# Attention of a decoder layer: turned heads split once and regrouped into stacks by SBUF transfers

## The reference

```python
kv = ln(x, kvn_w, kvn_b) @ kv_w + kv_b              # 16 heads of 32, keys and values
q  = ln(x, qn_w, qn_b) @ q_w + q_b
q, k = rotary(q, x, rh_w, rh_b), rotary(k, x, rh_w, rh_b)   # scaled by a radius that depends on the row
qn, kn = ln(q, ln_w, ln_b), ln(k, ln_w, ln_b)        # over the 32 of a head
attn = softmax(einsum('bhqd,bhkd->bhqk', qn, kn) / sqrt(32))
x1 = x + einsum('bhqk,bhkd->bhqd', attn, v) @ out_w + out_b
```

## Time and profile before

| | us |
|---|---|
| median of 3 runs | 2368.12 (2367.32 to 2368.73) |
| time of the profiled execution | 2366.49 |
| its span, from first to last instruction | 2364.7 |
| mean granted clock of PE over the span, as a share | 0.926 |

### The profile page before, as it was taken

How to read it: one execution, slowest core, us unless ns; L and a number is a source line. 1 busy time by engine, 2 the same in 40 slices (tenths; PEclk the granted TensorE clock), 3 DMA queues, 4 the chain that set the end, 5 groups by cost and what they waited for, 6 DMA issues and landing times. The chain is left out here.

```text
span 2364.7 us, 31908 instructions
## 1 busy us (share of the span) xinstructions
PE 1990.4 (84%) x10328; PEld 1432.6 (61%) x10328; DVE 1609.8 (68%) x3007; ACT 1061.1 (45%) x1820; POOL 1025.8 (43%) x879
## 2 busy tenths in 40 slices
PE   4579989899898989989984999999948887878872
PEld 4446656665665656656533888887837666666651
DVE  4467777777777777877744666767544777777765
ACT  1246546464563645646552222222215456555653
POOL 1568668587685876858610222222101212222121
PEclk9689999999999999999987999999969999999885
DMA  3000010100001010010104121111031121022111
GB/s 131 0 28 1 15 42 1 55 1 28 28 1 55 1 31 25 1 36 1 36 1 171 41 87 53 53 53 53 19 111 36 54 72 56 15 71 72 54 36 54
DMA packets 54718, 99.24 MB, mean 42 GB/s; under 512 B 5040, under 2 KB 8112, under 8 KB 54576
## 3 DMA queue, kind: packets, MB, share of 16 engines
q1 hardware_dynamic: 54576, 97.38, 12.0%
HBM read 63.82 MB, written 33.55 MB: 41 GB/s over the span
## 5 line engine op out<-in xcount | busy, mean ns | idle before, releaser
L438 DVE TENSOR_REDUCE a_neg_max<-a_max 128x1 f32<-128x512 f32 x512 | 341.5, 686 | 146.0 <-PE a_max L702 143.2
L594 ACT ACTIVATE a_probs<-a_exp 128x512 f32<-128x512 f32 x512 | 285.4, 596 | 288.8 <-PE a_exp L717 285.8
L1421 POOL TENSOR_TENSOR f_mixed<-f_tw,f_beta 128x512 f32<-128x512 f32 x64 | 96.1, 1521 | 343.2 <-DVE f_beta L1520 169.3
L294 POOL TENSOR_TENSOR a_rstd<-a_rstd,a_minus_half 128x16 f32<-128x16 f32 x64 | 186.3, 2911 | 121.8 <-DVE a_rstd L423 121.8
L702 PE MATMUL a_max<-a_stack 96*128 96x512 f32 x512 | 232.4, 457 | 6.7 <-DVE a_neg_max L438 6.4
L580 ACT ACTIVATE a_stack<-a_exp 96x512 fp32r<-96x512 f32 x256 | 138.4, 590 | 140.3 <-PE a_exp L689 139.6
L674 PE MATMUL a_t<-a_w_hi,a_zT_hi 128*128 128x384 f32 x512 | 176.5, 345 | 29.0 <-DVE a_v L406 29.0
L717 PE MATMUL a_exp<-a_stack 100*128 100x512 f32 x512 | 186.8, 407 | 5.4 <-ACT a_probs L594 3.4
L702 PEld LDWEIGHTS a_max<-a_stack 96*128 96x128 f32 x512 | 98.4, 193 | 145.9 <-issue 81.1
L971 POOL TENSOR_TENSOR r_part<-r_part 128x512 f32<-128x512 f32 x32 | 45.8, 1431 | 313.8 <-DVE r_part L1018 313.8
L689 PE MATMUL a_exp<-a_ident,a_n 128*96 128x128 f32 x1024 | 142.8, 283 | 43.3 <-ACT a_stack L580 35.1
(11 more groups left out here) (239 smaller groups left out, 5220.0 us busy)
## 6 DMA issues: line engine op xcount, KB each, us to landing
a_z<-x SPq DMA_DIRECT2D x8, 1024.0 KB, 5.6
a_y<-x SPq DMA_DIRECT2D x32, 256.0 KB, 2.7
x<-a_y SPq DMA_DIRECT2D x32, 256.0 KB, 2.2
r_xn<-x SPq DMA_DIRECT2D x8, 1024.0 KB, 5.6
r_cn<-ctx SPq DMA_DIRECT2D x8, 1024.0 KB, 7.7
x<-r_xn SPq DMA_DIRECT2D x8, 1024.0 KB, 4.3
f_xn<-x SPq DMA_DIRECT2D x8, 1024.0 KB, 5.5
x<-f_xn SPq DMA_DIRECT2D x8, 1024.0 KB, 7.2
```

The source lines that it names most:

```text
L294: nc.gpsimd.tensor_tensor(rstd[:, c], rstd[:, c], minus_half[:, :], ALU.pow).then_inc(pool_step, 1)
L438: nc.vector.tensor_reduce(neg_max[:, t, ROW + h:ROW + h + 1], bank_max[i % 2][:, :], AX_X, ALU.max, negate=True).then_inc(max_done, 1)
L594: nc.scalar.activation(probs[:, kt % 2, h, :], bank_exp[i % 2][:, :], ACT.Exp, scale=float(1.0 / np.sqrt(np.float32(HD)))).then_inc(exp_do ...
```

## The change

Only `attention_phase` changes. In the reader's order:

1. **Heads are turned once.** PE transposes each side's normed heads (`turn_heads`, 4 transposes a side, all four heads in 128 rows) into `bank_t`. ACT takes the high part (`turn_high`), DVE the low one (`turn_low`). n3, its copies, `make_stack` and `save_stack` are gone.
2. **Stacks are put together by transfers.** SP issues 24 of them for each unit (`regroup`), SBUF to SBUF, each of 32 partitions by 512 float32 (64 KB), six for each head, with a semaphore for each head. It waits for the low parts of both sides and for the last key scores that read the same half of `stack`. Query scores of head h wait for its six.
3. **Head norm weights on the query side only.** The products' weight is squared and its bias multiplied once at the start, and the key side gets neither. The key side comes first (`SIDES`).
4. **Order of PE.** Query scores are done by step 13, key scores run from step 1 to 12, the four weighs stand in the unit's own steps 5, 8, 11 and 14 as pairs of values and sums, the maxima are turned at step 14 and `save_max` follows there, projection stands at steps 0 to 8, and the two sides are turned at 9 and 11. DVE does quarters 0 and 1 of normalise at step 15 and quarters 2 and 3 at 0 and 1 of the next unit.
5. **x over several units.** Its load is issued in g = 1 for two batches on; statistics run in g = 2, their end (`x_final`, `x_shift`) in g = 3; ACT normalises (`x_norm`) in g = 0, where PE turns the tiles too, now in `bank_t`, between the tiles of the output's projection. All of them share two banks and wait for one another.
6. **Output.** y has four tiles and one transfer in and one out for each batch; POOL adds the bias (`add_bias`) in g = 2 and 3.

```diff
+QS_DONE = tuple(T * HG * min(i + 1, 14) // 14 for i in range(16))
+KS_DONE = tuple(T * HG * min(i, 12) // 12 for i in range(16))
+PROJECT_DONE = (3, 5, 6, 8, 10, 11, 13, 15, 16, 16, 16, 16, 16, 16, 16, 16)
+WEIGH_AT = (5, 8, 11, 14)
+TURN_AT, SAVE_AFTER = (9, 11), (2, 4, 7, 9)
+OUT_AT, ADD_AFTER, OUT_BANK = (10, 12, 15, 15), (11, 13, 15, 15), (1, 1, 0, 1)
+Z_AT, Z_HIGH_AT, Z_LOW_AFTER = (13, 13, 14, 14), (13, 13, 15, 15), (13, 14, 15, 15)
+MAX_AT, SAVE_MAX_AT = 14, 14
+X_NORM_AT, STATS_AFTER, FINAL_AFTER, SHIFT_AFTER = (5, 6, 7, 8), (6, 8, 10, 12), 6, 12
+MEAN_AFTER, VAR_AFTER, SQUARE_AT = (0, 1), (3, 4), (1, 2)
+TURN_HIGH_AT, TURN_LOW_AFTER = (10, 12), (11, 13)
+NORM_AFTER, ATTN_HIGH_AT, ATTN_LOW_AFTER = (15, 15, 0, 1), 2, 3
+SIDES = (1, 0)
...
+            def regroup(U, par):
+                if counts(U - 1):
+                    sp.wait_ge(keyscore_done, T * HG * (U - 1))
+                sp.wait_ge(nTlo_done, 2 * U + 2)
+                for h in range(HG):
+                    src = slice(h * HD, (h + 1) * HD)
+                    for j, c, parts in ((h, 0, (nT_hi, nT_lo, nT_hi)), (HG + h, 1, (nT_hi, nT_hi, nT_lo))):
+                        for r, part in enumerate(parts):
+                            sp.dma_start(stack[r * HD:(r + 1) * HD, par, j, :].bitcast(F32), part[src, c, :].bitcast(F32)).then_inc(stacked[h], 16)
...
+            def unit(b, g, left, more):          # SP
+                if left >= 2:
+                    regroup(G * b + g + 2, g % 2)
+                if g == 0 and counts(b):
+                    sp.wait_ge(y_sum, T * (b + 1))
+                    sp.dma_start(rows(x1, b - 1), y[:, :, :]).then_inc(x1_out, 16)
+                if g == 1:
+                    if counts(b):
+                        sp.wait_ge(x1_out, 16 * b)
+                    sp.dma_start(y[:, :, :], rows(x, b)).then_inc(y_in, 16)
...
+            def turn_low(U, s, bank):
+                c = SIDES[s]
+                dve.wait_ge(nThi_done, 2 * U + s + 1)
+                nc.vector.tensor_tensor(nT_lo[:, c, :], bank[:, :], nT_hi[:, c, :].bitcast(F32),
+                                        ALU.subtract).then_inc(nTlo_done, 1)
...
+            def turn_high(U, s, bank):
+                c = SIDES[s]
+                act.wait_ge(nT_done, 2 * U + s + 1)
+                if s == 0 and counts(U):
+                    for h in range(HG):
+                        act.wait_ge(stacked[h], 6 * 16 * U)
+                nc.scalar.activation(nT_hi[:, c, :], bank[:, :], ACT.Copy).then_inc(nThi_done, 1)
...
-            def unit(b, g, left, first=False):   # ACT
-                    save_stack(U + 1, (g + 1) % 2, m)
+            def unit(b, g, left, more):
+                U = G * b + g
+                for i in range(T * HG):
+                    for m in within(KS_DONE, i):
+                        exps(U, m)
+                    if i == ATTN_HIGH_AT and counts(U):
+                        attn_hi(U - 1, (g - 1) % G)
+                    for s in range(2):
+                        if left >= 2 and i == SQUARE_AT[s]:
+                            square(U + 2, s)
+                        if left >= 2 and i == TURN_HIGH_AT[s]:
+                            turn_high(U + 2, s, bank_t[0 if g == 0 else s])
+                    for t in range(T):
+                        if g == 0 and left == 4 and i == X_NORM_AT[t]:
+                            x_norm(b + 1, t)
+                        if g == 0 and left == 4 and i == Z_HIGH_AT[t]:
+                            z_high(b + 1, t)
+                    if i == SAVE_MAX_AT and left >= 1:
+                        save_max(U + 1, (g + 1) % 2)
...
             def query_scores(U, par, i):
                 if t == 0:
-                    pe.wait_ge(stack_saved, 2 * (HG * U + h + 1))
+                    pe.wait_ge(stacked[h], 6 * 16 * (U + 1))
...
+            def turn_heads(U, s, bank):
+                c = SIDES[s]
+                pe.wait_ge(n_done, 2 * U + s + 1)
+                for t in range(T):
+                    last = nc.tensor.transpose(bank[:, t * P:(t + 1) * P],
+                                               n[:, c, t * HG:(t + 1) * HG, :].rearrange("p h i -> p (h i)"), ident[:, :])
+                last.then_inc(nT_done, 1)
...
+            def unit(b, g, left, more):          # PE
+                for i in range(T * HG):
+                    if left >= 1:
+                        for m in within(QS_DONE, i):
+                            query_scores(U + 1, (g + 1) % 2, m)
+                    if left >= 3:
+                        for m in within(PROJECT_DONE, i):
+                            project_item(b, g, left, m)
+                    for m in within(KS_DONE, i):
+                        key_scores(U, g % 2, m)
+                    if i in WEIGH_AT:
+                        weigh(U, g, WEIGH_AT.index(i))
+                    if i == MAX_AT and left >= 1:
+                        transpose_max(U + 1)
+                    for s in range(2):
+                        if left >= 2 and i == TURN_AT[s]:
+                            turn_item(b, g, left, s)
+                    for t in range(T):
+                        if g == 0 and left == 4 and i == Z_AT[t]:
+                            z_item(b, t)
+                    for t in range(T):
+                        if g == 0 and counts(b) and i == OUT_AT[t]:
+                            out_item(b, left, t)
```

More of the change, by code:

```diff
@@ L215, in _ @@
                 sp.dma_start(dst, src).then_inc(load_w, 16)
[L217 to L233, removed]
+            sp.wait_ge(zT_done, T)
+            sp.dma_start(z[:, :, :], rows(x, 1)).then_inc(x_in, 16)
             sp.wait_ge(w_low, 2 * K)
@@ L237, in _ @@
             sp.dma_start(raw_out, w["out_w"].rearrange("(k p) n -> p k n", p=P)).then_inc(load_out, 16)
[L238 to L245, removed]
+            regroup(0, 0)
+            regroup(1, 1)
+            run(sp, unit)
+            sp.wait_ge(y_sum, T * (B + 1))
+            sp.dma_start(rows(x1, B - 1), y[:, :, :]).then_inc(x1_out, 16)
+            sp.wait_ge(x1_out, 16 * B)
         @block.gpsimd
@@ L304, in unit, with add_bias @@
+                last.then_inc(n_done, 1)
+            def add_bias(b, t):
+                pool.wait_ge(y_in, 16 * (b + 1))
+                nc.gpsimd.tensor_tensor(y[:, t, :], y[:, t, :], out_bias[:, :], ALU.add).then_inc(y_biased, 1)
+            def unit(b, g, left, more):
                 U = G * b + g
                 if left >= 2:
[L306 to L309, removed]
@@ L327, in _ @@
-            run(pool, unit, steps, 12 * G)
+            nc.gpsimd.tensor_tensor(head_b[:, :], head_b[:, :], head_w[:, :], ALU.mult).then_inc(pool_step, 1)
+            pool.wait_ge(pool_step, steps.next())
+            nc.gpsimd.tensor_tensor(head_w[:, :], head_w[:, :], head_w[:, :], ALU.mult).then_inc(pool_step, 1)
+            pool.wait_ge(pool_step, steps.next())
+            for s in range(2):
+                rotate(0, s)
+            for U in range(2):
+                for s in range(2):
+                    centre(U, s)
+                for s in range(2):
+                    head_norm(U, s)
+                if U == 0:
+                    x_rstd(1)
+                for s in range(2):
+                    rotate(U + 1, s)
@@ L329, in _ @@
+            run(pool, unit, steps, POOL_STEPS)
         @block.vector
@@ L490, in unit @@
                     if left >= 3 and i in SAVE_AFTER:
                         save_qkv(U + 3, (g + 3) % G, SAVE_AFTER.index(i))
-                    if new_x and i in STATS_AFTER:
-                        x_stats(b + 1, STATS_AFTER.index(i))
+                    for s in range(2):
+                        if left >= 2 and i == TURN_LOW_AFTER[s]:
+                            turn_low(U + 2, s, bank_t[0 if g == 0 else s])
+                    if g == 2 and more and i in STATS_AFTER:
+                        x_stats(b + 2, STATS_AFTER.index(i))
@@ L494, in unit @@
+                    if g == 3 and more and i == FINAL_AFTER:
+                        x_final(b + 2)
+                    if g == 3 and more and i == SHIFT_AFTER:
+                        x_shift(b + 2)
+                    for t in range(2):
+                        if g == 0 and counts(b) and i == ADD_AFTER[t]:
+                            add_out(b - 1, t)
                     for t in range(T):
-                        if g == 0 and not first and i == ADD_AFTER[t]:
+                        if g == 0 and left == 4 and i == Z_LOW_AFTER[t]:
+                            z_low(b + 1, t)
@@ L496, in unit @@
+                    for t in range(2, T):
+                        if g == 0 and counts(b) and i == ADD_AFTER[t]:
                             add_out(b - 1, t)
-                    if new_x and i == T * HG - 1:
-                        normalise_x(b + 1)
+                    for c in range(T):
+                        if i == NORM_AFTER[c] and i >= 8:
+                            normalise(U, c)
             for t in range(T):
```

(3 more changed lines are left out.)

497 lines of the change are left out of this document (232 added, 265 removed).

## The result

The changed kernel takes 2424.6 us (median of 4 runs, 2422.6 to 2433.0), the kernel before 2368.4 in the same comparison: a ratio of 1.0245, 95% interval 1.0219 to 1.027. It is slower, by 56 us. The forecast was 2335, faster by 33, with a range of 2285 to 2388: the change went the other way, and the time lies above the range. The profiled execution took 2423.0, its span 2421.0.

What follows compares the result with a forecast made beforehand. PE was taken to bound ordinary units, and a DVE, PE, ACT, DVE chain the turning of z. Six batches -7.8, start -13, batch 0's units 1 to 3 +5.1, last batch -17.8: -33.5, so 2335 us, range 2285 to 2388.

Steps and rivals of the forecast that it cites:

- Turn_low at 26.5: In an ordinary unit, DVE finishes the query side's low part 26.5 us after the unit's first query score.
- the wait on a landing at the seam as such: Ahead of an ordinary unit's first query score, PE stands empty for 3 us until head 0's transfers land.
- g = 0 with its two stalls: Unit g = 0 ends at 45.3 us, with z tiles waiting 1.9 on turn_low and output tile 2 waiting 2.6.
- Rival A: The forecast itself: the wait before each unit's first query score is bound by transfers; 2310 to 2360 us, chance 0.55.
- They are covered; so are the other 18 issues on SP, whose other work (y, x) stands behind them: Transfers for heads 1 to 3 come 2.6 us apart, needed at 7, 14 and 20, so they cost nothing.
- Issues at 0.44: Head 0's six transfers are issued on SP 0.44 us apart; with a landing of 2.0 they take 4.3.
- half the seams pay: Half the waits before a unit's first query score drop PE's clock: 0.4 us a unit, 1.0 in g = 0.
- rival C: Every wait before a unit's first query score drops PE's clock for 4 to 8 us: 2375 to 2417, chance 0.22.
- PE's own 25.8, and 27.8 without transfers: In an ordinary unit PE's own work is 25.8 us; with waits for DVE but no transfers, 27.8.
- g = 1 absorbs 2 of 3.3: DVE enters g = 1 behind 3.3 us of add_out and two quarters; its idle time takes back 2: unit 32.1.
- The last batch: Its units g = 0 to 3 take 38.5, 28.5, 19.4 and 15.0 us: -17.8 in all.
- The phases behind: Phases after attention, which the diff does not touch, are taken as unchanged.

Runs made afterwards that it cites:

- the two kernels with five issues: Loads first, keys early, early turn and high part first, with head 0's high-part transfers merged: 2335.3 us; then two of the five issues moved to ScalarE: 2333.8 us.
- the filler run: Kernel after plus 14 matmuls nobody reads at the end of each unit of g = 1, 2, 3, where PE would stand idle: 2413.7 us, ratio 1.0181.

## Why the prediction was wrong, by its steps

Between the profiled executions -33.5 was forecast and +56.5 came, a miss of 90. By place: units 1 to 3 of batch 0 took 105.7 where 96.3 was forecast, +9.4; the six batches +42.7 where -7.8 was, +50.5; the last batch +2.1 for -17.8, +19.9; the phases behind, taken as unchanged, +10.0.

By units of the six batches, as means and with the forecast's clock: g = 0 46.05 for 46.3, g = 1 35.6 for 32.5, g = 2 37.1 for 32.5, g = 3 32.3 for 31.3. The largest miss is in g = 2, the next in g = 1.

**Right.** Turn_low at 26.5 (26.6 in the unit with g = 3), PE's last work at 27.8 (27.9 there), landing 2.0, the wait on a landing at the seam as such, and g = 0 with its two stalls, though the terms named for its 45.3 (25.8, 11.3, 2.2, 1.9 and 2.6) add up to 43.8. Rival A named the mechanism; its size did not hold. That unit 1 starts at 157.98, for 158.1 by the steps, is luck in part: the first unit was 2.2 shorter than forecast (32.7 for 34.9) and began 2.0 later (125.25 for 158.1 - 34.9).

**"They are covered; so are the other 18 issues on SP, whose other work (y, x) stands behind them".** This is the step that failed. The sentence named the queue and not the wait: 24 issues are 15 us of SP, the load behind them is needed by VectorE in the next unit, and VectorE is in PE's loop. Five of the six g = 2 units have this load to wait for and took 37.5 to 39.4; with the two loads ahead of the transfers they took 33.5 to 34.3, so 3.2 to 5.9 of each is this wait. The move gave 33 us back. (The sixth, in the batch that neither loads z nor takes its statistics, took 31.6; it does not bear out the 32.1, which has the statistics in it.)

**Issues at 0.44.** Mis-sized: the row was of two loads of 256 KB, the pitch of the small transfers is 0.63. The five gaps are 3.1 in place of 2.2, which is the 0.9 by which the seam of 3.85 exceeds the forecast 3. Three issues fewer behind the low part took 43 us off. The estimate of 2.15 for one transfer, from the fit in the Trainium skill (DMA: Bandwidth & Descriptors, section Anatomy of one DMA), agrees with the 2.0 measured.

**The clock, "half the seams pay", 0.4 a unit.** Mis-sized: every one of the 17 such seams between 300 and 1150 is followed by 8 to 15 slow projection matmuls, at 0.50 for the first 3.47 us of the unit with g = 3 shown above. That is rival C's condition, and its time (2375 to 2417) was the nearest, though 2424.6 lies above it too. The clock is not the bulk of the loss: up to the end of attention the same 5600 matmuls keep PE busy for 1060.1 in the kernel after and for 1033.3 without transfers, so the falls that go with the seams lengthen them by some 27 us, where the step costs 99. Behind the wait of 5.05 the clock is at the lower level; the Trainium skill (TensorE: Matmul & The Clock Gate, Part 1: The HAM clock gate) calls the throttled state the default, released by activity, and the trace agrees.

**PE's own 25.8, and 27.8 without transfers.** Mis-sized: the run without transfers shows 27.0 to 27.4 of busy time and units of 29.1 to 29.5. The 27.8 is met only where there is a seam, in which VectorE has time to catch up; the difference is hidden as long as the seam is there, and is what stops the repaired kernels at 2334. My own count of the tie (score i waits for row_max i - 2) was right in kind and too small.

**g = 1 absorbs 2 of 3.3.** It did not: SP's first issue there is at 31.0 of the unit, where 32.1 has it at 27.8, and the unit is 35.6 as a mean for 32.5. Some 1.4 of that is the clock: the units with 11 or 12 slow matmuls take 35.9 to 36.2, the one with none 34.7. This fall is not the seam's. Without transfers it is there too, behind a wait for a row maximum that the kernel after also has (1.61 there), and the unit takes 32.0, against 30.6 in the one batch where the clock holds:

```profile
575.60 0.80 PE L727 MATMUL a_max<-a_stack 96*128 96x512 f32 x1 [1.60 <-DVE a_neg_max L465]
576.20 0.52 PE L701 MATMUL a_t<-a_w_hi,a_zT_hi 128*128 128x384 f32 x1
```

**The last batch.** g = 0 took 39.5 (38.5). g = 1 took 34.2 (28.5): the seam is in it. g = 2 took 25.7 to its first key score (19.4), where a half-speed stretch, row maxima and 2.0 for save_max lie, and g = 3 with the output projection behind it 42.0 (35.1, the forecast 15.0 and the 20.1 that the last projection took before).

**The phases behind.** The forecast took them as unchanged. The retention phase took 450.6 for 449.2 on PE, the coupling phase 592.8 for 585.2, with the same instructions. The batch of the coupling phase that differs most, before and after:

```profile
1999.60:2070.60 71.00, 57.77 (x241) 44.69 (x241) 51.08 (x97) 40.30 (x70) 14.48 (x10) 0.90 0.17 59
```

```profile
2048.80:2124.50 75.70, 56.99 (x241) 44.27 (x241) 51.02 (x97) 40.29 (x70) 14.52 (x10) 0.91 0.17 56
```

The busy times agree, the length does not. Most of the 10 us stands in this batch, ahead of one instruction of VectorE, before and after:

```profile
2005.70 0.69 DVE L1470 TENSOR_REDUCE f_sums<-f_w 128x4 f32<-128x512 f32 x1 [1.04 <-ACT f_xT_hi L1593]
```

```profile
2061.32 0.69 DVE L1546 TENSOR_REDUCE f_sums<-f_w 128x4 f32<-128x512 f32 x1 [7.39 <-issue]
```

Nothing in the profile releases the pause of 7.39. All 12 experiments have it ahead of the same instruction (6.3 to 7.4), and their phases behind attention are 6 to 12 us longer than before, whatever their attention phase did. Four packets of an instruction queue fall into this batch in the kernel after and none in the kernel before; no run tested whether they make the pause, and its cause is open. The phases behind also vary by up to 5 us between the experiments, so a difference of that size between two kernels says little of attention. In the profiled executions attention alone ends 98.8 us earlier without transfers, 32 with the loads first, 36 with the keys early and 25 with the early turn.

## What to carry over

When a copy is moved from an engine to transfers, count three things: the pitch of the issues ahead of the first that is needed, what is queued behind the last of them, and which engine waits for that. Two queue entries in the wrong order cost a third of what the whole step cost. And a stall hides the next bound: price the step by leaving it out (99 us here) before repairing it, since what is behind (row maxima here, 46 us) will stop the repair. With the loads first, head 0's keys early and an earlier turn the plan is 1.4% faster than the kernel before (2336.6 us, ratio 0.9862), and with 20 issues on two queues 1.5% (2333.8), the fastest of the kernels that compute the whole result. A filler that keeps an engine busy is a test of the clock only where no other wait takes up the gain.

## What the runs showed of the hardware

- An issue on SP's queue of 64 KB, 32 partitions of SBUF to SBUF, takes 0.59 us, 0.63 from one to the next (24 of them 15.1), against 0.44 for each of two loads of 256 KB and 0.39 for a load of a megabyte. A transfer lands 2.0 us after its issue; one of 128 KB, 2.4.
- The granted clock fell to 0.50 behind each of the 17 waits of 3.9 to 5.1 us. Shorter waits don't sort by length: behind 1.8 to 3.2 us it fell at some seams and not at others; in the kernel with loads, keys and turn early it fell behind waits of 0.6 to 0.9 us at five starts of g = 3, and in the two kernels with five issues, at seams of up to 1.4, at none. It fell behind the same two waits of 1.4 and 1.6 us for a row maximum in five of six g = 1 units and held in the sixth, with and without transfers, and in the filler run behind pauses of 2.5 us of PE.
- In the coupling phase VectorE paused for 6.3 to 7.4 us ahead of one and the same instruction in all 13 kernels with the changed attention phase, and not in the kernel before; the code of that phase is the same in all of them.
